# Edge matrix of a graph kernel: the places of a batch packed four to a word, and loaded during the batch ahead

## The reference

```python
# x: 3125 x 256, fp32; 50000 edges (src, dst, weight), dst sorted
h = acc = layernorm(x)
for _ in range(3):
    h = segment_sum(weight[:, None] * h[src], dst, 3125)
    h = h / max(norm(h), 1e-12)          # row by row
    acc = acc + h
x = x + acc / 4
# then: layernorm, a gate with the two best of 16 experts, their two matmuls,
# the weighted sum, a residual and a layernorm with gamma and beta
```

## Time and profile before

| | |
|---|---|
| median of 3 runs | 1495.72 us (1495.12 to 1513.82) |
| the profiled execution | 1496.09 us, span of its trace 1494.3 us |
| PE busy | 1289.3 us (86%) |
| DVE busy | 1081.0 us (72%) |
| ACT busy | 893.2 us (60%) |
| tables | 0 to 49.4 us |
| edge matrix | 49.4 to about 400 us, its last store to 418 us |
| layers | from 400.8 us to about 1090 us |

### The profile page before, as it was taken

The page is one execution under the profiler, slowest core; times in us unless marked ns, Lnnn a source line. Parts: engine busy times, 40 slices in busy tenths (PEclk is TensorE's granted clock), DMA queues, the critical chain, the costliest instruction groups (busy, mean ns, idle before and its releaser), DMA issues. The chain is left out here.

```text
span 1494.3 us, 31330 instructions
## 1 busy us (share of the span) xinstructions
PE 1289.3 (86%) x9561; PEld 1141.9 (76%) x9562; DVE 1081.0 (72%) x1893; ACT 893.2 (60%) x1985; POOL 258.4 (17%) x232
## 2 busy tenths in 40 slices
PE   4576777777799999999999999999886999898995
PEld 1476776666678888888888888888753998898975
DVE  8998898898676665666665666665475788887847
ACT  1788888888755555555555555555432666555663
POOL 1300000000040000000000000000002688887620
PEclk9899999999999999999999999999985999998998
DMA  5388888888886666666666666656322787787763
GB/s 188 77 204 201 206 202 195 201 204 209 212 266 190 185 184 184 177 187 184 185 183 183 178 178 184 184 174 194 96 88 86 222 257 240 240 257 213 246 209 124
DMA packets 236493, 283.03 MB, mean 189 GB/s; under 512 B 16269, under 2 KB 173045, under 8 KB 236421
## 3 DMA queue, kind: packets, MB, share of 16 engines
q1 hardware_dynamic: 228741, 261.28, 63.2%
q0 software_dynamic: 7680, 20.98, 4.4%
HBM read 194.27 MB, written 87.93 MB: 189 GB/s over the span
## 5 line engine op out<-in xcount | busy, mean ns | idle before, releaser
L852 PE MATMUL ps_rows<-h_both,a_high 128*128 (+1 forms) x1875 | 505.5, 397 | 13.3 <-DVE h_both L696 5.6
L691 DVE TENSOR_TENSOR a_low<-a_raw,a_high 128x640 fp32r<-128x640 f32 x375 | 305.4, 823 | 234.2 <-ACT a_high L585 230.9
L585 ACT ACTIVATE a_high<-a_raw 128x640 fp32r<-128x640 f32 x375 | 274.5, 740 | 288.3 <-PE ps_rows L855 264.1
L852 PEld LDWEIGHTS ps_rows<-h_both,a_high 128*128 128x128 f32 x1875 | 329.5, 190 | 71.9 <-ACT halves L599 14.5
L855 PEld LDWEIGHTS ps_rows<-h_both,a_low 128*128 128x128 f32 x1875 | 275.6, 190 | 32.7
L829 PE MATMUL ps_w<-lo_hot,key_w 128*120 128x160 bf16 x2736 | 218.4, 238 | 92.7 <-issue 70.0
L855 PE MATMUL ps_rows<-h_both,a_low 128*128 (+1 forms) x1875 | 284.4, 283 | 0.0
L829 PEld LDWEIGHTS ps_w<-lo_hot,key_w 128*120 128x120 bf16 x2736 | 206.1, 136 | 100.4 <-issue 100.1
L567 ACT ACTIVATE win<-ps_w 128x480 f32<-128x480 f32 x304 | 148.6, 575 | 47.9 <-PE ps_w L834 31.7
L675 DVE TENSOR_TENSOR key_w<-key_hot,tab_marks 128x1440 bf16<-128x1440 bf16 (+1 forms) x228 | 164.4, 775 | 0.0
L558 ACT ACTIVATE key_w<-key_hot,third_b 128x120 bf16<-128x120 bf16 x456 | 141.4, 420 | 5.4 <-DVE key_hot L666 3.0
(11 more groups left out here) (244 smaller groups left out, 1649.8 us busy)
## 6 DMA issues: line engine op xcount, KB each, us to landing
a_raw<-a_rows SPq DMA_DIRECT2D x375, 320.0 KB, 3.2
a_rows<-win SPq DMA_DIRECT2D x228, 240.0 KB, 3.6
w_raw<-in_L_ffn_w SPq DMA_DIRECT2D x80, 512.0 KB
a_rows<-win SPq DMA_DIRECT2D x76, 180.0 KB
b_t<-in_L_ffn_b SPq DMA_DIRECT2D x40, 128.0 KB
found<-results SPq DMA_DIRECT2D x6, 640.0 KB, 8.6
hf<-in_x SPq DMA_DIRECT2D x1, 3072.0 KB
x<-in_x SPq DMA_DIRECT2D x1, 3072.0 KB
```

The source lines that it names most:

```text
L585: a.activation(a_high[:, u, :], a_raw[:, u, :], ACT.Copy).then_inc(high_split, 1)
L691: v.tensor_tensor(a_low[:, u, :], a_raw[:, u, :], a_high[:, u, :].bitcast(F32), ALU.subtract).then_inc(low_split, 1)
L852: nc.tensor.matmul(ps[:, banks[w][r], :], a_high[:, u, r * P:(r + 1) * P], both, start=first, stop=False, skip_group_check=True)
```

## The change

The places are counted in grains of 32 columns (160 columns are 5 grains, a bank has 16), so that a field needs 6 bits, and four fields go into one word. The place of a batch's first step is always 0, and its field is left out: 11 places and the slot are 12 fields in 3 words. In the tables, the clearing of `fields` goes, `fields` is written without the first place, and three multiply-adds over 76 x 3 elements pack it where one over 76 x 8 did.

On PE, two sets of three registers are held across batches. A batch's three words are loaded by PE's sequencer behind the sixth of the twelve steps (LOAD_AT = 5) of the batch that comes first; those of batch 0 before the batches begin. The load between the L810 matmuls and the first L829 matmul goes. A field is now cut out by a mask and a shift (the top one of a word by a shift alone).

```diff
-        self.ROW = 8
-        self.FIELD = 2048
+        self.WORDS = -(-self.BATCH // 4)
+        self.ROW = 4
+        self.FIELD = 64
+        self.GRAIN = 32
...
-            link(v.memset(fields[:], 0.0))
-            v.tensor_scalar(fields[:, :, B], moved[:], float(B), float(s.LO), ALU.min, ALU.mult)
+            v.tensor_scalar(fields[:, :, B - 1], moved[:], float(B), float(s.LO // s.GRAIN), ALU.min, ALU.mult)
...
-            v.scalar_tensor_tensor(tab.place[:], fields[:, :, 1::2], float(s.FIELD), fields[:, :, 0::2],
-                                   ALU.mult, ALU.add)
+            for k in (2, 1):
+                link(v.scalar_tensor_tensor(fields[:, :, k::4], fields[:, :, k + 1::4], float(s.FIELD),
+                                            fields[:, :, k::4], ALU.mult, ALU.add))
+            v.scalar_tensor_tensor(tab.place[:, :, 0:s.WORDS], fields[:, :, 1::4],
+                                   float(s.FIELD), fields[:, :, 0::4], ALU.mult, ALU.add)
...
+            held = [[pe.alloc_register(f"places_{u}_{n}") for n in range(s.WORDS)] for u in range(2)]
+
+            def load_places(b, u):
+                pe.reg_load(held[u], tab.place[0:1, one(b), 0:s.WORDS].rearrange("p b w -> p (b w)"))
+
+            load_places(0, 0)
+
             def multiply(b, i):
+                words = [nc.snap(r) for r in held[i % 2]]
...
-                words = nc.values_load_multi_w_load_instructions(
-                    tab.place[0:1, one(b), :].rearrange("p b w -> p (b w)"), engines=[mybir.EngineType.PE], min_val=0,
-                    max_val=s.FIELD ** 2 - 1,
-                    skip_runtime_bounds_check_because="two fields of eleven bits each")[1]
-
-                def field(j, top):
-
-                    value = words[j // 2] >> 11 if j % 2 else words[j // 2] & (s.FIELD - 1)
+                def field(n, top):
+
+                    word = words[n // 4]
+                    low = 6 * (n % 4)
+                    value = word >> low if n % 4 == 3 else (word & ((s.FIELD - 1) << low)) >> low
...
-                places = [field(j, (BANKS - 1) * 512 + (PER - 1) * LO) for j in range(B)]
-                slot = field(B, B * LO)
+                top = ((BANKS - 1) * 512 + (PER - 1) * LO) // s.GRAIN
+                places = [slice(0, GRAINS)] + [bass.DynSlice(field(j, top), GRAINS) for j in range(B - 1)]
+                slot = bass.DynSlice(field(B - 1, B * GRAINS), GRAINS)
...
                 for j in range(B):
                     for k in range(3):
...
+                    if j == LOAD_AT and (not isinstance(b, int) or b + 1 < NB):
+                        load_places(b + 1, 1 - u)
```

More of the change, by code:

```diff
@@ L129, in phase_tables @@
         fresh = sb("fresh", [1, s.NB])
-        fields = sb("fields", [1, s.NB, 2 * s.ROW])
+        fields = sb("fields", [1, s.NB, 4 * s.WORDS])
         stats = sb("stats", [P, CH, 6])
@@ L301, in _ @@
             floor_div(v, link, bank[:], slot[:], s.PER_BANK)
-            link(v.tensor_scalar(bank[:], bank[:], float(512 - s.PER_BANK * s.LO), None, ALU.mult))
-            link(v.scalar_tensor_tensor(fields[:, :, 0:B], slot[:].rearrange("p (b j) -> p b j", j=B), float(s.LO),
-                                        bank[:].rearrange("p (b j) -> p b j", j=B), ALU.mult, ALU.add))
-            v.scalar_tensor_tensor(tab.place[:], fields[:, :, 1::2], float(s.FIELD), fields[:, :, 0::2],
-                                   ALU.mult, ALU.add)
+            link(v.tensor_scalar(bank[:], bank[:], float((512 - s.PER_BANK * s.LO) // s.GRAIN), None, ALU.mult))
+            link(v.scalar_tensor_tensor(fields[:, :, 0:B - 1], slot[:].rearrange("p (b j) -> p b j", j=B)[:, :, 1:B],
+                                        float(s.LO // s.GRAIN), bank[:].rearrange("p (b j) -> p b j", j=B)[:, :, 1:B],
+                                        ALU.mult, ALU.add))
+            for k in (2, 1):
[3 more added lines that the diff above has]
+                                   float(s.FIELD), fields[:, :, 0::4], ALU.mult, ALU.add)
         @block.tensor
@@ L353, in phase_layers @@
         WIDE = PER * LO
+        GRAINS = LO // s.GRAIN
         PAIRS = B // 2
@@ L382, in phase_layers @@
         PAD_AT = 14
+        LOAD_AT = 5
         PADDING = -(-(CH * P) // CW) - s.W
@@ L811, in multiply @@
                        start=True, stop=False, skip_group_check=True)
-                words = nc.values_load_multi_w_load_instructions(
-                    tab.place[0:1, one(b), :].rearrange("p b w -> p (b w)"), engines=[mybir.EngineType.PE], min_val=0,
-                    max_val=s.FIELD ** 2 - 1,
-                    skip_runtime_bounds_check_because="two fields of eleven bits each")[1]
-                def field(j, top):
-                    value = words[j // 2] >> 11 if j % 2 else words[j // 2] & (s.FIELD - 1)
+                def field(n, top):
+                    word = words[n // 4]
+                    low = 6 * (n % 4)
+                    value = word >> low if n % 4 == 3 else (word & ((s.FIELD - 1) << low)) >> low
                     return nc.s_assert_within(value, min_val=0, max_val=top,
                                               skip_runtime_bounds_check_because="made of a slot up to B")
-                places = [field(j, (BANKS - 1) * 512 + (PER - 1) * LO) for j in range(B)]
-                slot = field(B, B * LO)
+                top = ((BANKS - 1) * 512 + (PER - 1) * LO) // s.GRAIN
+                places = [slice(0, GRAINS)] + [bass.DynSlice(field(j, top), GRAINS) for j in range(B - 1)]
+                slot = bass.DynSlice(field(B - 1, B * GRAINS), GRAINS)
+                sums = ps_w[0:M, u, :].rearrange("p (q e) -> p q e", e=s.GRAIN)
+                kept = win[:, (i - 1) % WINS, :].rearrange("p (q e) -> p q e", e=s.GRAIN)
                 pe.wait_ge(hot_ready, (b + 1) * 4)
@@ L828, in multiply @@
                     for k in range(3):
-                        ins = mm(ps_w[0:M, u, bass.DynSlice(places[j], LO)], key_w[:, u, k, j // 2, :, j % 2],
+                        ins = mm(sums[:, places[j], :], key_w[:, u, k, j // 2, :, j % 2],
                                  lo_hot[:, u, j // 2, :, j % 2],
                                  start=False, stop=False, skip_group_check=True)
+                    if j == LOAD_AT and (not isinstance(b, int) or b + 1 < NB):
+                        load_places(b + 1, 1 - u)
                 if late(b, 1):
                     pe.wait_ge(windows_out, b)
-                    ins = mm(ps_w[0:M, u, bass.DynSlice(places[0], LO)], ident[:, 0:M],
-                             win[:, (i - 1) % WINS, bass.DynSlice(slot, LO)],
+                    ins = mm(sums[:, places[0], :], ident[:, 0:M],
+                             kept[:, slot, :],
                              start=False, stop=False, skip_group_check=True)
                 ins.then_inc(multiplied, 1)
-            batches(pe, multiply)
+            for b in range(2 * WINS):
+                multiply(b, b % WINS)
+            with pe.Fori(2, NB // WINS - 1) as it:
+                for i in range(WINS):
+                    multiply(it * WINS + i, i)
+            for i in range(WINS):
+                multiply(NB - WINS + i, i)
             def step(layer, w, c, u, first, last):
```

## The result

The changed kernel takes 1541.91 us (median of four runs, 1534.32 to 1547.39) against 1499.26 for the kernel before beside it: a ratio of 1.0271, 95% interval 1.0226 to 1.0316. It is 43 us slower, where 1494 was forecast.

A forecast was written before the change was run, and what follows sets the result against it. The prediction took SP's chain of stores, about 4.5 us a batch, to bound the edge matrix. Its terms summed as 1496.1 + 0 + 0 - 2.4 = 1493.7, so 1494 us, with an 8-in-10 range of 1477 to 1512.

The forecast's parts named there:

- How long a load takes: PE's load in the edge matrix: 0.03 us a word, so three words for eight are worth -0.14 us.
- 3.0 us and a load: PE's step in the edge matrix: the load in the middle stays mostly exposed, beside 3.0 us of other sequencer work.
- The register work: Cutting out packed fields on PE: longer fused instructions add +0.3 us a batch, between -0.1 and +0.6.
- its own 4.7: PE's step in us, 3.0 + 0.3 + 1.58 - 0.14, if the load kept its median; 4.0 with a load of 0.8.
- PE becomes the bound: Edge matrix: PE's step exceeds SP's 4.585 us; 1505 us at 4.7, 1520 at 4.9, 1542 at 5.2; chance 0.24.
- The stores' own pace: SP's store chain in the edge matrix keeps about 4.5 us a batch whatever PE does: 1488 to 1500 us, chance 0.55.
- It was the load after all: Edge matrix: the queue hides PE's load and stores follow DVE's 3.97 us: -45 us, 1451 us; chance 0.06.
- the stores get quicker: Edge matrix: SP's load falls to 0.49 us and the DMA engines follow, -19 us, 1477 us; chance 0.15.
- The only term that counts: Change of SP's pace in the edge matrix as PE's load moves: half of -4.9 us, so -2.4 us.
- SP waits for windows: Sign in the edge matrix that PE has become the bound, refuting that the stores have a pace of their own.
- Tables and first load: Before the batches: DVE ends 1.0 us earlier, covered by POOL, cost 0; first load 0, at most 0.65 us.
- The gap in the middle: L829 idles in the middle of its 36 matmuls, behind 18, instead of before them: the load mostly exposed there.

The follow-up runs named there:

- the place alone: Kernel before, eight words of two fields, but with held registers and the load behind the sixth step: 1502.98 us, ratio 1.0014.
- the packed fields with two pieces: Changed kernel with table rows of eight words (five of them 0), all eight loaded: 1511.63 us, ratio 1.0081.
- no load: Changed kernel, all batches using batch 0's words, so no load follows in the batches: 1499.08 us, ratio 0.998.
- a fourth word: Changed kernel loading four words, three used: 1499.69 us; the same with packed fields loaded between the batches, as before: 1498.07 us.
- SP's loads gone too: Changed kernel with PE loading four words, three used, and SP loading its window numbers for four batches at once: 1489.97 us, ratio 0.9962.
- the load behind the last step: Changed kernel with the load behind the last of the twelve steps instead of the sixth (LOAD_AT = 11): 1543.59 us, ratio 1.0258.
- seven words: Kernel before, but PE loads only the seven words it uses instead of the row of eight: 1580.1 us, ratio 1.0558.
- the packing alone: Changed kernel's three packed words, but loaded between the batches as in the kernel before: 1551.4 us, ratio 1.0311.
- four batches in one load: Changed kernel, places of four batches (sixteen words) fetched in one load behind every fourth batch's last matmul: 1525.35 us, ratio 1.0154.
- the ninth word: Kernel before with held registers and the load behind the sixth step, loading nine words, the ninth unused: 1535.05 us, ratio 1.0215.

## Why the prediction was wrong

**The step that failed is "How long a load takes".** From two rows (8 words 0.65 us on PE, one word 0.46 us on SP) it made a line of 0.03 us a word, and from it -0.14 us for three words. Two points on two engines were joined by a straight line, and the cost isn't one in words: it goes by pieces, two before and three after. Nor were the points free of traffic, as the step says. The 0.65 was read at 60.3 us, behind SP's first store issue at 59.89; the 0.46 at 405 to 413 us, while the DMA engines were 0.90 busy:

```profile
400.00:418.00 18.00, 15.92 (x80) 13.73 (x81) 9.70 (x20) 8.29 (x19) 0.00 (x0) 0.88 0.90 239
```

By themselves, one word takes 0.32 us, eight take 0.60 and three 0.77: +0.17 in place of -0.14, and the sign is wrong. Among the stores a piece costs more: in the middle of the batch the median is 0.83 us for one, 1.17 and 1.34 for two, 1.46 and 1.57 for three. Against the 1.34 of the place alone, -0.14 would have been 1.20; it was 1.46. The step also said that "the rest of the 1.58 us is the stores' traffic and stays"; the loaded time grows with the pieces, too.

**In the sum, the load's term came out right by luck.** The prediction had 3.3 + 1.44 = 4.7 for PE's step; it was 3.57 + 1.46 = 5.03. The new place had taken 0.24 us off the median of eight words (1.58 to 1.34), which had no term, and the third piece put about as much back. The sum's miss of 0.29 stands in the rest, where the forecast had kept PE's step at "3.0 us and a load": with held registers and the middle place alone the rest is 3.35. Two rows account for an increase of that size, though no experiment separates them. In the kernel of the place alone PE copies eight held registers for each batch (39 of 53 copies stand at this line):

```profile
L813 PEldq FUSED_REGOPS  x39: 140/140/140, 111.0 to 346.5; - x39
```

And the 36 matmuls, which took 2.80 us in one run, take two runs of 1.50 us, one on each side of the load, in that kernel's timeline. Either fault alone costs less than half of the loss: with the load at 1.20, the step of 3.57 + 1.20 = 4.77 would have cost 75 x (4.77 - 4.585) = 14 us by the rival's own arithmetic, and the packed fields with two pieces, whose load is 1.17 and step 4.79, were measured at 12 us.

**The register work was right in size and too small beside the rest.** +0.3 us was forecast. Summed over the traces' rows, all of PE's fused instructions and ALU_OPs take 1.19 us a batch before and 1.46 after, +0.27. Of that, the fields' cutting itself is less than forecast (L829's 0.97 against L844's 1.13, +0.16), and the copying of three held registers, for which there was no term, is another 0.08. By experiment, packed fields against the place alone, the rest of PE's step grows from 3.35 to 3.63.

**The prediction then chose against its own 4.7**, which by its own arithmetic is 1505, on the ground that the load's median "belongs to a PE that waits for a load among the last stores' issues" and that loads had taken as little as 0.70. That ground is refuted: with PE as the bound and the stores thinner (issues 0.45 us, DMA share 0.83), the median was still 1.46. This choice is what turned a warning into a chance of 0.24.

**The rival "PE becomes the bound" happened, with its own arithmetic.** It put the turn at 4.585 us for the step; at 5.03 it gives 1496.1 + 75 x (5.03 - 4.585) = 1529, and the profiled execution took 1534.3. It would decide "once a load takes more than 1.3 us"; the median is 1.46. Its price of 1542 was for a step of 5.2; that the measured median is 1542 too is a coincidence.

**The stores' own pace was right.** SP's period is 4.53 us with no load on PE and 4.58 with a fourth word, and 1498 to 1500 us is the time in three kernels that differ from each other on PE (no load, a fourth word in two places). "It was the load after all" (1451) is refuted by the same runs, as is most of "the stores get quicker": PE's load gone wholly changed nothing measurable, and with SP's loads gone too the median is 6 us lower, hardly clear of the noise. "The only term that counts", SP's pace with its -2.4, counted for nothing, since SP was no longer the bound. My sign for a refutation, "SP waits for windows", was drawn too wide: SP does wait for them, and the stores have their pace all the same. The two paces lay so near each other that one piece of a load changed which of them rules.

**Tables and first load** came out otherwise than said, without weight for the result. The packing takes 1.64 us for two multiply-adds and 0.80 for the third, where 1.2 was forecast for all three, so DVE ends at 48.07, 0.12 us earlier and not 1.0:

```profile
45.60 1.64 DVE L308 SCALAR_TENSOR_TENSOR fields<-fields 1x228 f32<-1x228 f32 x2
47.27 0.80 DVE L310 SCALAR_TENSOR_TENSOR tab_place<-fields 1x228 int32<-1x228 f32 x1
```

POOL covers that, as forecast. Batch 0's load takes 0.96 us at 52.1, before the batches, and SP's first store issue comes at 61.50 in place of 59.89, 1.6 us later where "at most 0.65" was said. With a fourth word it comes at 60.15, and nothing is seen of it at the layers' start (400.89 against 400.80).

**The gap in the middle** came out as said: the load in the middle is exposed for 1.37 us behind 18 matmuls. The Trainium skill's queue of 64 for TensorE ("TensorE: Matmul & The Clock Gate") hides next to nothing here, in the middle (a load of 1.38 us) or, as the load behind the last step shows, at the end (a gap of 1.49 us, where the loads' median is 1.61).

## What to carry to other kernels

Before a load is made shorter, measure loads of the old and the new size by themselves in the kernel's quiet stretch; a row of 4 aligned words can be cheaper than 3, and a spare word is worth its place. Where two chains run at the same period, work out both steps and the margin between them (here 4.7 us, by the forecast's own sum, against the stores' 4.585): when the sum puts the other engine above the bound, that belongs in the likeliest case. Loads behind one another are not only their sum: here four short stops cost less than one long one (1500 us against 1525).

## What the runs showed that was not expected

- A register load's time on PE with no store about: 0.32 us for 1 word, 0.55 for 2, 0.77 for 3, 0.34 for 4, 0.62 for 5, 0.84 for 6, 1.05 for 7, 0.60 for 8, 0.86 for 12 and 1.10 for 16; from a start that isn't divisible by four, 1.01 for 4.
- The same load among the stores: one piece 0.33 becomes 0.83 us in the median, three pieces 0.77 become 1.46 to 1.99, four pieces 1.05 become 2.50 (seven words) and 1.10 become 3.27 (sixteen words, behind the batch).
- PE's granted clock wasn't the same in kernels with the same matmuls. From 105 to 350 us it was 1.00 with a fourth word, 0.98 before, 0.95 after, and with seven words 0.87:

```profile
105.00:350.00 245.00, 165.43 (x1815) 159.84 (x1812) 175.12 (x218) 168.16 (x480) 0.00 (x0) 0.87 0.73 164
```

So part of what a longer load costs is matmuls at the lower of the two clock levels behind it. In the kernel with seven words PE stood idle for 3.07 us, and its next 36 matmuls took 5.05 us; those of the batch behind took 2.79:

```profile
209.40 5.05 PE L829 MATMUL ps_w<-lo_hot,key_w 128*120 128x160 bf16 x36 [3.07 <-ACT key_w L558]
215.18 2.79 PE L829 MATMUL ps_w<-lo_hot,key_w 128*120 128x160 bf16 x36
```

```profile
209.00:215.00 6.00, 5.60 (x42) 5.49 (x42) 1.82 (x3) 1.40 (x5) 0.00 (x0) 0.50 0.84 198
```

By the starts of the matmuls in the traces, one follows another after 73 to 81 ns at a granted clock of 1.00 and after some 134 ns at 0.50, the lower level (1.2 GHz). Counting those at the lower level gives an estimate of what the clock took in the edge matrix: 4 us before, 10 after, 42 with seven words, 22 with the packing alone, 18 with four batches in one load; and 11 with the ninth word against 2 with the place alone. So some 6 of the 43 us that the change lost, about a quarter of the third piece's price, and nearly half of the 84 us of seven words are the clock's. It follows the stops on PE and is no cause beside them: with a fourth word the estimate is 3 us.
